# Table entries written a chunk later, the last chunk's routing moved ahead, and one identity for three stages

## What is computed

```python
# attention: 16 heads of 32, causal; keys and values through a latent of 128
x = x + attention(layernorm(x)) @ wo_w + wo_b
# feed-forward: a shared expert, and the two best of 8 experts for each token
h = layernorm(x)                              # no scale, no shift
probs = softmax(h @ gate_w.T)                 # 8 experts
topk_w, topk_ids = top_k(probs, 2); topk_w /= sum(topk_w)
routed = sum over the two experts e of  topk_w * ((silu(h @ w_gate[e]) * (h @ w_up[e])) @ w_down[e])
shared = (silu(h @ sw_gate) * (h @ sw_up)) @ sw_down      # inner width 352
out = x + routed + shared
```

## Time and profile before

| | before |
|---|---|
| median of three runs | 2542.58 us |
| profiled execution | 2533.65 us, its span 2532.1 us |
| TensorE (PE) busy | 2301.3 us, 91% of the span |
| VectorE (DVE) busy | 1515.1 us, 60% |
| ScalarE (ACT) busy | 1042.6 us, 41% |
| GpSimd (POOL) busy | 1189.4 us, 47% |
| stage C | 1484.7 to 1894.0 us after the span's start |
| its chunk 0 | from 1521.87 to 1566.62 us |
| its chunks 1 to 6 | from 1566.62 to 1839.87 us |
| its last chunk and the end of the stage | from 1839.87 to 1894.0 us |

### The profile page before, as it was taken

One profiled execution on the slowest core, in us unless ns is written; L12 is line 12 of the kernel. 1 busy time (PEld: TensorE's weight loads), 2 busy tenths in 40 slices (PEclk: granted clock), 3 DMA queues, 4 the chain that ended last, 5 costly groups with the idle time before them and its releaser, 6 DMA issues. The chain is left out here.

```text
span 2532.1 us, 33323 instructions
## 1 busy us (share of the span) xinstructions
PE 2301.3 (91%) x11973; PEld 1450.3 (57%) x11973; DVE 1515.1 (60%) x3317; ACT 1042.6 (41%) x1925; POOL 1189.4 (47%) x765
## 2 busy tenths in 40 slices
PE   5998499999999999999999959999959999999997
PEld 5776244444444444444444336776747878788786
DVE  2665587677767677776767345555535555555553
ACT  2333045555555555555555632122113343333332
POOL 0000036566665656566565764344343544444543
PEclk8999599999999999999999979999979999999999
DMA  3766711313123131513121023343236656566561
GB/s 104 264 234 237 169 34 35 84 34 84 35 51 84 35 87 37 141 40 84 39 51 53 24 70 113 110 140 100 84 117 196 200 185 205 176 191 216 178 161 34
DMA packets 171610, 285.98 MB, mean 113 GB/s; under 512 B 30137, under 2 KB 72633, under 8 KB 171456
## 3 DMA queue, kind: packets, MB, share of 16 engines
q1 hardware_dynamic: 145152, 210.45, 28.5%
q0 software_dynamic: 26304, 73.54, 9.7%
HBM read 198.61 MB, written 92.38 MB: 115 GB/s over the span
## 5 line engine op out<-in xcount | busy, mean ns | idle before, releaser
L848 ACT ACTIVATE b_pt<-b_st 128x512 f32<-128x512 f32 (+3 forms) x1280 | 612.6, 535 | 485.5 <-DVE b_st L810 205.6
L665 POOL TENSOR_TENSOR b_acc<-b_acc,b_pt 128x1024 f32<-128x1024 f32 (+1 forms) x256 | 592.8, 2345 | 213.3 <-ACT b_pt L848 213.1
L789 DVE TENSOR_REDUCE b_mpart<-b_mx 128x1 f32<-128x512 f32 x768 | 512.3, 686 | 199.2 <-PE b_mx L905 196.7
L926 PE MATMUL b_st<-b_q,b_k 97*128 97x512 f32 (+2 forms) x1280 | 496.6, 401 | 74.8 <-ACT b_pt L848 54.6
L905 PE MATMUL b_mx<-b_k,b_q 96*128 96x512 f32 (+2 forms) x1280 | 508.1, 412 | 29.9 <-DVE b_mt L797 25.9
L905 PEld LDWEIGHTS b_mx<-b_k,b_q 96*128 96x128 f32 x1280 | 248.1, 195 | 284.4 <-DVE b_mpart L789 153.2
L926 PEld LDWEIGHTS b_st<-b_q,b_k 97*128 97x128 f32 x1280 | 241.8, 190 | 281.2 <-ACT b_pt L848 240.0
L939 PE MATMUL b_ob<-b_pt,b_v 128*32 128x512 f32 (+3 forms) x2560 | 302.2, 544 | 1.1 <-ACT b_pt L848 1.1
L786 DVE CUSTOM_DVE_ANT_0 b_unread<-b_mx,b_later 128x384 bf16<-128x384 f32 (+3 forms) x512 | 245.0, 485 | 89.2 <-PE b_mx L905 88.8
L665 POOL TENSOR_TENSOR b_acc<-b_pt 128x1024 f32<-128x1024 f32 x48 | 113.4, 2379 | 299.7 <-ACT b_pt L848 299.5
L69 PE MATMUL e_fb<-e_xh,e_w_guh 128*128 128x512 f32 (+1 forms) x552 | 220.4, 399 | 1.5 <-DVE e_xl L1744 1.5
(11 more groups left out here) (228 smaller groups left out, 3529.9 us busy)
## 6 DMA issues: line engine op xcount, KB each, us to landing
b_q<-scr_qh SPq DMA_DIRECT2D x64, 256.0 KB, 4.6
b_k<-scr_kh SPq DMA_DIRECT2D x64, 256.0 KB, 4.1
sw_gu<-in_L_ffn_w_gate_dram SPq DMA_DIRECT2D x12, 704.0 KB
sw_gu<-in_L_ffn_w_up_dram SPq DMA_DIRECT2D x12, 704.0 KB
a_xin<-in_L_attn_x_dram POOLq DMA_DIRECT2D x8, 1024.0 KB, 5.9
scr_qh<-a_qh SPq DMA_DIRECT2D x8, 1024.0 KB, 4.5
scr_ql<-a_ql SPq DMA_DIRECT2D x8, 1024.0 KB, 6.8
scr_kh<-a_kh SPq DMA_DIRECT2D x8, 1024.0 KB, 5.2
```

Source lines behind the costliest of these rows:

```text
L665: g.tensor_tensor(out[:, :, lo:], so_far[:, :, lo:], pt[n % NPB][:, :, lo:], ALU.add).then_inc(s_add, 1)
L789: v.tensor_reduce(part, mxb[i % NMX][:, 0:w], AX.X, ALU.max).then_inc(s_red, 1)
L848: act.activation(pt[n % NPB][:, j, lo:], stb[:, (2 * n + j) % NST, lo:], ACT.Exp, scale=SCALE).then_inc(s_exp, 1)
L926: pe.matmul(stb[:, (2 * n + j) % NST, lo:], kb[:, h, at:at + P], qb[:, h, q * CH + lo:(q + 1) * CH], start=True, stop=True).then_inc(s_st, 1)
```

## The change

1. GpSimd's `before_norm` is cut into `normalize` (the product and the additions) and `deviation`; `place_entries` into `second_weight` (L1242) and the table DMAs. The loop now runs: normalise chunk c+1, table DMAs of chunk c-1, second weight of c, deviation of c+1; the last table DMAs follow the loop.
2. In the last chunk VectorE takes the logits and chooses before slice 0, and does slots and map_blocks between slices 0 and 1. TensorE turns the logits between the gate and the up product of slice 0, and makes counts and positions before slice 1.
3. One identity matrix, made in stage B, serves stages B, C and E. GpSimd makes none in C and E and TensorE doesn't wait for one.
4. The gather of block 1's rows moves from the end of stage C to the start of stage E.

```diff
-                def before_norm(c, first=False):
+                def normalize(c, first=False):
                     if not first:
                         g.wait_ge(s_o, c * 80)
                     g.tensor_tensor(on[:], oin[:], rin[:], ALU.mult).then_inc(s_on, 1)
...
                     ins.then_inc(s_xw, 1)
+
+                def deviation(c):
                     wait_apart(g, s_var, c * TPC + TPC, s_gpass)
...
-                def place_entries(c):
+                def second_weight(c):
                     g.wait_ge(s_gap, c + 1)
                     if c:
                         g.wait_ge(s_slot, c)
                     g.tensor_tensor(ex[:], euler[:], gap[:], ALU.pow).then_inc(s_ex, 1)
+
+                def place_entries(c):
                     g.wait_ge(s_slot, c + 1)
...
-                g.wait_ge(s_cst, 3)
-                before_norm(0, first=True)
+                g.wait_ge(s_cst, 1)
+                normalize(0, first=True)
+                deviation(0)
                 route_constants()
                 for c in range(NCH):
                     if c + 1 < NCH:
-                        before_norm(c + 1)
-                    place_entries(c)
+                        normalize(c + 1)
+                    if c:
+                        place_entries(c - 1)
+                    second_weight(c)
+                    if c + 1 < NCH:
+                        deviation(c + 1)
+                place_entries(NCH - 1)
                 g.wait_ge(s_xst, NCH * 16)
                 g.wait_ge(s_ol, NCH)
-                g.wait_ge(s_x1, NCH * TPC)
-                for b in range(2):
-                    g.wait_ge(keep["entries_in"][b], 16)
-                    gather_rows(g, keep, scratch["xn"], b, keep["x"][b], keep["x_in"][b])
+                g.wait_ge(keep["entries_in"][0], 16)
+                gather_rows(g, keep, scratch["xn"], 0, keep["x"][0], keep["x_in"][0])
...
                 def step(c, first=False, last=False):
                     if last:
                         expert_rows(c)
-                    hidden(c, 0, first)
-                    if not last:
+                        token_rows(c)
+                        choose(c)
+                        hidden(c, 0)
+                        slots(c)
+                        map_blocks()
+                        hidden(c, 1)
+                    else:
+                        hidden(c, 0, first)
                         expert_rows(c)
                         o_low(c + 1)
                         hidden(c, 1, first)
-                    token_rows(c, first)
-                    choose(c)
-                    if last:
-                        hidden(c, 1, first)
-                        map_blocks()
-                        slots(c)
-                    else:
+                        token_rows(c, first)
+                        choose(c)
                         residual(c + 1)
                         norm(c + 1)
...
                 def counts():
+                    pe.wait_ge(s_both, NCH)
                     pe.matmul(lb[:, CNT:CNT + E], all_ones[:], sooner[NCH % 2][:, 0], start=True, stop=True).then_inc(s_cnt, 1)
...
                         logits(c)
-                    hidden(c, 0, first)
-                    if last:
+                        hidden(c, 0, both=[0])
                         turn_logits(c)
+                        hidden(c, 0, both=[1])
+                        counts()
+                        positions(c)
+                        hidden(c, 1)
                     else:
+                        hidden(c, 0, first)
                         logits(c, first)
-                    hidden(c, 1, first)
-                    if not last:
+                        hidden(c, 1, first)
                         turn_logits(c)
                         att(c + 1)
-                    positions(c)
-                    if last:
-                        counts()
+                        positions(c)
                     hidden(c, NF - 1, first)
...
             def _(g):
-                make_identity(g, ident, s_cst, 0)
-
                 def scatter(b):
...
+                g.wait_ge(keep["entries_in"][1], 16)
+                gather_rows(g, keep, scratch["xn"], 1, xg[1], s_x[1])
                 gather_rows(g, keep, out, 0, rows[0], s_r[0])
```

More of the change, by code:

```diff
@@ L512, in batch_rows, with phase_attention @@
     return scratch[name][b * CPB:(b + 1) * CPB].rearrange("c h t -> (c h) t")
-def phase_attention(nc, x, w, scratch, ahead):
+def phase_attention(nc, x, w, scratch, ahead, keep):
     units, steps, first_step = attention_steps()
@@ L584, in phase_attention @@
         al = Alloc(nc, ctx)
-        ident = al.sb("b_ident", [P, P])
+        ident = keep["ident"]
         ones = al.sb("b_ones", [P, DH])
@@ L1050, in phase_shared @@
         al = Alloc(nc, ctx)
-        ident = al.sb("c_ident", [P, P])
+        ident = keep["ident"]
         mhalf = al.sb("c_mhalf", [P, TPC])
@@ L1533, in counts, with hidden @@
                 def counts():
+                    pe.wait_ge(s_both, NCH)
                     pe.matmul(lb[:, CNT:CNT + E], all_ones[:], sooner[NCH % 2][:, 0], start=True, stop=True).then_inc(s_cnt, 1)
-                def hidden(c, f, first=False):
-                    for which in range(2):
+                def hidden(c, f, first=False, both=range(2)):
+                    for which in both:
                         n = 2 * f + which
@@ L1554, in down_rows @@
                             ins.then_inc(s_dn, 1)
-                pe.wait_ge(s_cst, 3)
                 pe.wait_ge(s_wl, 1)
@@ L1619, in phase_experts @@
         al = Alloc(nc, ctx)
-        ident = al.sb("e_ident", [P, P])
+        ident = keep["ident"]
         wt = [FfnWeights(al, "e_w0", ahead.raw), FfnWeights(al, "e_w1")]
@@ L1635, in parts @@
             return [(wt[n].gu[:, j], wt[n].guh[:, j], wt[n].gul[:, j]) for j in range(2)] + wt[n].down_parts()
-        s_cst = al.sem("e_constants_made")
         s_w = keep["weights_in"]
@@ L1798, in step @@
                         down(nc, fb[t][:], wt[n], hh, hl, t, [NF - 1]).then_inc(s_dn, 1)
-                pe.wait_ge(s_cst, 2)
                 transposes(0, 0, range(KD), True)
@@ L1831, in program @@
         keep = {
+            "ident": al.sb("ident", [P, P]),
             "expert": al.sb("expert", [P, NB], I32),
@@ L1839, in program @@
         }
-        phase_attention(nc, x, w, scratch, ahead)
+        phase_attention(nc, x, w, scratch, ahead, keep)
         phase_shared(nc, x, w, scratch, ahead, keep)
```

## The result

| | before | changed |
|---|---|---|
| median | 2538.66 us | 2552.15 us |
| ratio | | 1.0059, 95% interval 1.0046 to 1.0072 |
| profiled execution, span | 2533.65 us, 2532.1 us | 2544.99 us, 2543.4 us |
| chunk 0 | 44.8 us | 49.9 us |
| chunks 1 to 6 | 273.25 us | 294.5 us |

Both medians are of ten executions (the 2542.58 further up was the median of three). One execution of the changed kernel (4653.53 us) and the profiled one of experiment e2 (2869.98 us) were slow ones; the ratios and the readings of traces leave them out.

The account below looks back on a forecast made before the run. TensorE plus its own queue's stalls was taken as the bound. The terms -0.6 - 14 - 13.4 + 42 gave +14 us, on 2542.58 a forecast of 2556.6 us; own range 2547 to 2566, 8 in 10 for 2519 to 2567.

Parts of the forecast that it names:

- What bounds the kernel: Shared stage, chunks 1 to 6: a step is TensorE's work plus its own queue's stalls, 17.5 us in six steps.
- (a) The heads: Starts of chunks 1 to 6: the product no longer waits behind table DMAs; 43.2 us a step, gain 14.
- the collision: Tails of the chunks: GpSimd's moved product and additions meet VectorE's slots() and hold its instructions, 42 us in sum.
- (b) The last chunk: End of the shared stage: earlier expert choice and entries, four gathers fewer; the stage ends 13.4 us earlier.
- cover: Last chunk: weight loads 4 us earlier and the store of acc done before the gathers; at most 1 us lost.
- (c) One identity: Stage starts: gain 0.6 us at the shared stage, between 0 and 0.7, and 0 in the expert stage.
- What the change adds: Chunk tails: product and additions start when the last rin load lands and delay x_low; 42 us, bounds 0 and 22.
- X: Time of x1's last residual in a step, from which the prediction counted the events of the tail.
- the first xn: Row cited for one-source VectorE instructions being held too: 0.92 us instead of 0.54 beside GpSimd's memsets.
- Rival 1: Chunk tails: only two-input VectorE instructions are held, tails cost 22.5 us in sum, time 2537 us; chance 0.27.
- Rival 2: Chunk tails: GpSimd and VectorE don't collide, all 28 us of gain stays, 2514.6 us; chance 0.17.
- Rival 3: Collision, but the last chunk gives less because its final wait is tied to stores; 2540 to 2566 us; chance 0.14.

Follow-up runs that it names:

- e2: The changed kernel with GpSimd's order as before, leaving the last chunk's rework, the moved gather and the one identity; 2524.44 us, ratio 0.9941.
- e1: The changed kernel with one wait added, so that GpSimd's product comes behind slots(); 2509.52 us, ratio 0.9892 to the kernel before.
- f6: e1 with the first expert's weight loads issued behind the two table reads instead of ahead of them; 2510.31 us, ratio 0.9894.
- f7: e1 with the four gathers of the second block back at the end of stage C; 2516.57 us, ratio 0.9903.
- p1: The changed kernel with GpSimd products, a memset and a one-input addition added after stage C, one VectorE form beside each; one execution, not timed for speed.

## Why the prediction held, step by step

**What bounds the kernel.** Right: TensorE plus the stalls of its queue. In e1, with the stalls gone, six steps are 258.4 us with TensorE busy 250.0.

**(a) The heads.** Forecast 259.2 us for chunks 1 to 6 without the collision, a gain of 14; e1 shows 258.4, a gain of 14.9, and the wait that remains is the one named, the residual's 1.1. Reading the new step off chunk 0, which had this order already, gave it within 0.2 us a step (43.2 forecast, 43.07 in e1).

**(b) The last chunk.** Forecast 13.4, measured 10.9. The first entry went out 14.0 us after the chunk's start instead of 22.7: 8.7 earlier, forecast 8.4. The failed step is "from first entry to reading the table is 13.0": it took 15.4. I had noted that the weight loads come 4 us earlier too, and booked it as cover. They did, by 3.7 us counted from the chunk's start, but the entries came 8.7 earlier and so changed places with them. Before, the loads were issued from 1861.43 to 1864.39 around the first entry at 1862.55, and the last entry, at 1871.70, ran alone; now they are issued 3.9 to 5.7 us behind the first entry, and the last four entries run among them. f6 shows that this is the cause (5.3 against 2.6 us to land). The first load before, then the changed kernel's entries, loads and gathers:

```profile
1861.43 0.41 SPq L1019 DMA_DIRECT2D sw_gu<-in_L_ffn_w_gate_dram  x1
```

```profile
1876.01 1.03 POOL L1252 DMA_INDIRECT scr_table<-c_entry,c_slot  x1 [3.90 <-DVE c_entry L1445]
...
1879.93 0.41 SPq L1019 DMA_DIRECT2D sw_gu<-in_L_ffn_w_gate_dram  x1
...
1891.41 0.36 SPq L1614 DMA_DIRECT2D entry<-scr_table  x1
...
1894.58 0.99 POOL L1607 DMA_INDIRECT oin<-scr_xn,entry  x1 [8.70 <-DMA entry<-scr_table]
...
1898.40 0.95 POOL L1607 DMA_INDIRECT oin<-scr_xn,entry  x1 [0.30 <-issue]
...
1905.24 1.38 ACT L1712 ACTIVATE e_w_guh<-sw_gu 128x1408 fp32r<-128x1408 f32 x1 [19.85 <-PEq L1150]
```

From the last gather to the next stage 6.84, forecast 7.16; from the table read to the first gather 3.17 instead of 2.44. So of the 2.5 us missing 2.4 are the table read and 0.7 the first gather; 0.3 more at the first entry and 0.3 at the end go the other way. TensorE is idle for 13.5 us here, where 12 were forecast and 26.0 stood before. The gathers moved into the next stage cost at most 1.4 us there (f7).

**(c) One identity.** 0.6 and 0 forecast, 0.6 and 0 measured.

**What the change adds.** Forecast 42, measured 42 in time (e1 to changed) and 41.1 in the traces (chunks 0 to 6, 344.5 against 303.4 us). With X as in the prediction (1693.85 in the tail shown): product at X+7.6, L1435 at X+7.84, x_low at X+17.6; forecast 7.6, 7.84 and 17.7. In the sum two sizes were off and cancelled, which is luck: the five tails of chunks 1 to 5 cost 7.2 each (294.5 less 258.4, by five), not 7.8, and the sixth, chunk 0's, 4.9 (49.9 less 45.0), where the sum had one tail of 3, for a late load. No load landed late enough to spare a tail; in two of them L1435 just slipped past the product (1602.99 against 1603.17), and the next one-input instruction, L1439, took its place with 4.3 us. The parts of the 7.2 were off as well: in chunks 1 to 6 the changed kernel has 24.6 us more of TensorE idle than e1 (33.0 against 8.4), 4.9 a tail where the prediction had a delay of 6.3, and 11.5 us more of it busy (261.5 against 250.0) on the same work at a lower granted clock (0.95 against 1.00), 2.3 a tail where it had 1.5.

One row behind the mechanism does not bear what was put on it. That one-input instructions are held was read off the first xn, 0.92 us beside GpSimd's memsets. It is L1439 to L1443 and p1 that show it, beside GpSimd work that reads SBUF; p1 has only a two-input form beside a memset, and that one was not held.

The Trainium skill ("SBUF — State Buffer", Who interferes with whom) says this: an exclusive lock for a whole instruction, taken by VectorE with two SBUF inputs and by copy, cast and tensor_scalar in their fast mode, never by reductions. The forms beside a product in experiment p1 agree, 3.5 to 3.7 us against 0.16 to 0.19; the hold of 2.63 us that ended before the one-input addition did does not fit "for a whole instruction".

**The rivals.** Rival 1 (only two-input instructions are held, 2537) fell with L1439 to L1443 and with p1. Rival 2 (no collision, 28 us below before) did not happen, but e1 is that case made on purpose: 26.8 us below before (2536.33 less 2509.52). Rival 3 was half right, in size and not in its reason: the last chunk gave 2.5 less, through the table read and not through stores: the last store of acc landed at 1897.4, 7.8 us before the next stage.

## What to carry to other kernels

Before moving work on GpSimd earlier, look at what VectorE runs at the new place. Ask which of its instructions read SBUF alone: beside GpSimd's product of 128x2048 each was held to that instruction's end, even one of four elements, while reductions, the reciprocal and PSUM readers passed. If the two must meet, put GpSimd behind VectorE's short serial chain (42 us here, for one wait) or cut its instruction in pieces (23 us here, although VectorE then gets in between them). And a transfer that a change moves has a neighbour at the new place too: the time to landing of what it now runs among is part of the sum.

## What the runs showed of the hardware that was not expected

- VectorE's PSUM readers did not feel the product at all: x_low took its 0.69 in the middle of it. I had counted only on which instructions are held; which are free decides where GpSimd's work can go.
- GpSimd's memset of 128x2048 did not hold a two-input instruction (0.16), its one-input addition did (2.63 us, ending 1.7 us before the addition). A one-input instruction beside a memset was not tried.
- One row stays unexplained: in p1 the last hl (L1392, alone 0.69) started at 1893.07, 0.48 us ahead of GpSimd's product, and yet took 5.62, while in the changed kernel an instruction 0.18 ahead of the product was through in 0.23. Which engine wins when both start within half a microsecond was not tried.
